# First query weights loaded in the key phase, the query products moved ahead of six value tiles, and their splits spread between value copies

## What is computed

```python
x = x + _L0_xattn_ref(_layernorm(x), ctx, ctx, Wq, Wk, Wv, Wd)
# inside: 32 query heads, 8 key/value heads, head size 128, 16 x 64 tokens, width 512
queries = _rope((q @ Wq.T).reshape(B, Sq, 32, 128).transpose(0, 2, 1, 3))
keys    = _rope((k @ Wk.T).reshape(B, Skv, 8, 128).transpose(0, 2, 1, 3))
values  = (v @ Wv.T).reshape(B, Skv, 8, 128).transpose(0, 2, 1, 3)
# then softmax(queries . keys) . values, times Wd, added to x
```

## Time and profile before

| | us |
|---|---|
| median of 3 runs (702.80 to 704.43) | 703.15 |
| the profiled execution | 705.12 |
| its span, first to last instruction | 703.1 |
| PE busy in that span | 693.3 (99%) |
| DVE busy | 517.9 (74%) |
| POOL busy | 471.2 (67%) |
| ACT busy | 371.7 (53%) |

### The profile page before, as it was taken

One profiled execution on the slowest core, in us unless ns is written; L12 is line 12 of the kernel. 1 busy time (PEld: TensorE's weight loads), 2 busy tenths in 40 slices (PEclk: granted clock), 3 DMA queues, 4 the chain that ended last, 5 costly groups with the idle time before them and its releaser, 6 DMA issues.

```text
span 703.1 us, 12868 instructions
## 1 busy us (share of the span) xinstructions
PE 693.3 (99%) x4841; PEld 563.6 (80%) x4841; DVE 517.9 (74%) x815; ACT 371.7 (53%) x560; POOL 471.2 (67%) x360
## 2 busy tenths in 40 slices
PE   8999999899999999999999999999999999999998
PEld 6887878678888888788788788887888888887886
DVE  5566898978768767767758758748658888899734
ACT  6356665734744743743752653654246777665220
POOL 2698155776787778778777877844525799985630
PEclk9999999999999999999999999999999999999999
DMA  7645513231310300311211212200300110010003
GB/s 264 213 151 176 163 61 89 91 141 43 116 49 16 134 30 27 122 45 48 87 45 60 75 45 76 76 16 2 104 2 1 46 32 32 2 64 29 16 1 119
DMA packets 25736, 51.08 MB, mean 73 GB/s; under 512 B 2400, under 2 KB 10720, under 8 KB 25696
## 3 DMA queue, kind: packets, MB, share of 16 engines
q1 hardware_dynamic: 25696, 50.53, 21.6%
HBM read 40.04 MB, written 10.49 MB: 72 GB/s over the span
## 4 chain that ended last, share of the span: by engine, by line
PE 85%; DVE 4%; POOL 4%; DMA 3%; issue 2%; ACT 1%; SPq 1%; POOLq 0%; DVEq 0%; ACTq 0%
PE pj L1733 13%; PE pj L1646 12%; PE pv L1733 10%; PE pj L1845 9%; PE tp L1646 9%; PE pj L2029 3%; PE pv L1632 3%; PE sc L1895 2%; PE tp L1908 2%; PE pv L1919 2%; PE pv L1720 2%; PE sc L1702 2%; PE tp L1709 2%; PE sc L1720 2%; POOL sm L506 2%
## 5 line engine op out<-in xcount | busy, mean ns | idle before, releaser
L500 POOL TENSOR_TENSOR sw<-sw,cst 128x512 f32<-128x512 f32 x72 | 97.0, 1347 | 41.9 <-ACT sw L685 41.7
L529 POOL TENSOR_TENSOR sm<-sm,rz 128x512 f32<-128x512 f32 x64 | 70.7, 1119 | 33.7 <-DVE rz L1259 33.7
L524 POOL TENSOR_TENSOR sm<-sm,mx 128x512 f32<-128x512 f32 x64 | 72.8, 1152 | 21.1 <-DVE mx L1253 13.4
L506 POOL TENSOR_TENSOR qr<-t,sw 128x512 f32<-128x512 f32 x54 | 73.8, 1367 | 7.8
L1646 PE MATMUL tp<-x,w 128*128 128x512 f32 x288 | 74.4, 395 | 0.0
L809 ACT ACTIVATE sm<-sm 128x512 f32<-128x512 f32 x64 | 40.1, 633 | 52.5 <-POOL sm L524 52.0
L518 POOL TENSOR_TENSOR w<-raw,w 128x896 fp32r<-128x896 f32 x24 | 50.3, 2117 | 25.9 <-ACT w L662 25.9
L1845 PE MATMUL pj<-xh,ws 128*128 128x512 f32 x192 | 64.6, 402 | 0.2 <-ACT kb L903 0.2
L1646 PEld LDWEIGHTS tp<-x,w 128*128 128x128 f32 x288 | 53.0, 188 | 10.7
L662 ACT ACTIVATE w<-raw 128x1792 fp32r<-128x1792 f32 x15 | 25.6, 1704 | 59.7 <-DVE raw L1113 59.7
L1257 DVE TENSOR_REDUCE zs<-sm 128x8 f32<-128x512 f32 x64 | 42.6, 666 | 14.0 <-ACT sm L809 13.7
(11 more groups left out here) (285 smaller groups left out, 1832.4 us busy)
## 6 DMA issues: line engine op xcount, KB each, us to landing
rawd<-in_w_d SPq DMA_DIRECT2D x16, 512.0 KB, 3.4
raw<-in_w_q SPq DMA_DIRECT2D x15, 512.0 KB, 3.3
kscr<-sm SPq DMA_DIRECT2D x16, 256.0 KB, 2.1
vscr<-sm SPq DMA_DIRECT2D x16, 256.0 KB, 2.6
kr<-kscr SPq DMA_DIRECT2D x8, 512.0 KB, 4.4
vv<-vscr SPq DMA_DIRECT2D x16, 256.0 KB, 3.4
raw<-in_w_v SPq DMA_DIRECT2D x4, 512.0 KB, 4.0
X<-in_x SPq DMA_DIRECT2D x4, 512.0 KB, 6.7
```

The costliest lines, as they stand in the source:

```text
L500: pool.tensor_tensor(bs(sw[par][:, :]), bs(sw[par][:, :]), rep(cst[:, C_SIN:C_SIN + S], HB), ALU.mult).then_inc(sin_done, 1)
L506: pool.tensor_tensor(o, bs(t1[par][:, :]), bs(sw[par][:, :]), ALU.add).then_inc(rope, 1)
L524: pool.tensor_tensor(s3, s3, per_group(mx[:, c, :], 8), ALU.subtract).then_inc(subbed, 1)
L529: pool.tensor_tensor(s3, s3, per_group(rz[:, c, :], 8), ALU.mult).then_inc(normed, 1)
```

## The change

It touches only the stretch up to the first head.

- The weights of query pair 0 are loaded into `raw8b` early, on SP's queue behind the loads of `X` and ahead of key pieces 4 and 5. Pair 1 then comes into `raw8`, pair 2 (`load_q(1, 0)`) into `raw8` too, so it waits for wlo 4 (both pairs split) where it waited for wlo 2.
- `PHASE1` ends behind value tile 9. Value tiles 10 to 15 stand behind the 14 products (before: 12 to 15).
- DVE: `stats_half(1)` comes one key tile earlier, the first two `ln_apply` three key tiles earlier, `w7_sum(0)` leaves the stretch between `ln_apply(5)` and `ln_apply(6)` and goes to key tile 7. The splits of weights and blocks behind it are put in another order. Both halves of `w7_lo(3, 1)` leave the first head and stand ahead of it, and `first_add(7)` stands ahead of `w7_sum(3)`.
- ACT: `w7_hi` and `block_hi` are spread over value copies 4 to 9.
- `t1f`'s third and fourth buffers lie in `kr` now, so `load_kr(0)` waits for all eight rope additions (rope Q0 + 8). It was free to load after wlo 4. The layer-norm temporaries move from `cq` to `swx`.

```diff
-         [("v", i) for i in range(5, 12)]
+         [("v", i) for i in range(5, 10)]
+V_LATE = 10
...
-        t1f, swf = t1 + [pt[0], t1x], sw + swx
+        t1f = t1 + [kr[:, i * HB:(i + 1) * HB, :].rearrange("p b s -> p (b s)") for i in range(2)]
...
             sp.dma_start(bthr[:, :], b_thr).then_inc(s_cols, 16)
+            load_q(0, 0, raw8b)
             for j in (4, 5):
...
-            sp.wait_ge(ln_t, NT)
-            load_q(0, 1, raw8b)
             for vi in range(6, NVT):
                 spill_v(vi)
                 if vi == 7:
-                    sp.wait_ge(wlo, 2)
-                    sp.wait_ge(wsum, 6)
+                    sp.wait_ge(wlo, 4)
                     load_q(1, 0)
                 if vi == 11:
                     for i in range(2):
                         sp.wait_ge(s_ks[i], 16 * NKT // 2)
-                    sp.wait_ge(wlo, 4)
-                    load_kr(0)
-                if vi == 12:
                     sp.wait_ge(wlo, 6)
                     load_q(1, 1)
+                    sp.wait_ge(rope, Q0 + 8)
+                    load_kr(0)
...
-                if ki in (5, 7):
-                    ln_pow((ki - 5) // 2)
+                if ki in (4, 5):
+                    ln_pow(ki - 4)
...
-                if ki in (3, 5):
-                    stats_half((ki - 3) // 2)
+                if ki in (3, 4):
+                    stats_half(ki - 3)
...
+                if ki == 7:
+                    w7_sum(0, raw8b)
...
+            for i in range(2):
+                w7_lo(0, 0, i, raw8b)
             block_lo(0)
...
+            w7_sum(1)
             block_lo(1)
-            w7_sum(1, raw8b)
             dve.wait_ge(ln_cp, NT)
             mix(0)
             mix(1)
-            for i in range(2):
-                w7_lo(1, 1, i, raw8b)
             block_lo(2)
             dve.wait_ge(tdone, 1)
             mix(2)
+            block_lo(3)
+            for i in range(2):
+                w7_lo(1, 1, i)
             dve.wait_ge(tdone, 3)
             mix(3)
+            block_lo(4)
             w7_sum(2)
-            block_lo(3)
-            block_lo(4)
...
             first_add(6, 6)
+            first_add(7, 7)
             w7_sum(3)
-            first_add(7, 7)
+            for i in range(2):
+                w7_lo(3, 1, i)
...
-                if first:
-                    w7_lo(3, 1, 0)
...
-                    w7_lo(3, 1, 1)
...
-            for i in range(12, NVT):
+            for i in range(V_LATE, NVT):
                 v_tile(i)
```

More of the change, by code:

```diff
@@ L121, in build @@
         wv1 = sb(p1, "wv1", [P, 2, KT, 512], F32R)
-        wk = [sb(p1, f"wk{i}", [P, 2, 2 * KT, P], F32R) for i in range(2)]
+        wk0 = sb(p1, "wk0", [P, 2, 2 * KT, P], F32R)
         sb(p1, "gap_p1", [P, 3 * 1024])
+        wk1 = sb(p1, "wk1", [P, 2, 2 * KT, P], F32R)
         wv0 = sb(p1, "wv0", [P, 2, KT, 512], F32R)
@@ L129, in build @@
         p1.close()
-        wv = [wv0, wv1]
+        wv, wk = [wv0, wv1], [wk0, wk1]
         f2 = ExitStack()
@@ L136, in build @@
         f2.close()
[L138 to L141, removed]
         pcb, u2b = sm4[0], sm4[1]
@@ L329, in ln_tmp @@
             if n < NT:
-                return cq[n % 2][:, :]
+                return swx[n % 2][:, :]
             return ((t1[1], sw[1], t1[0], sw[0]), sm4)[n // NT - 1][n % 4][:, :]
@@ L341, in build @@
         FIRST = [(0, 0), (1, 0), (0, 1), (1, 1), (0, 2), (1, 2), (0, 3), (1, 3)]
-        t1f, swf = t1 + [pt[0], t1x], sw + swx
+        t1f = t1 + [kr[:, i * HB:(i + 1) * HB, :].rearrange("p b s -> p (b s)") for i in range(2)]
+        swf = sw + swx
         block = es.enter_context(nc.Block())
@@ L408, in _ @@
                     sp.wait_ge(plo_d, 7)
-                    load_q(0, 0)
+                    sp.wait_ge(wsum, 1)
+                    load_q(0, 1)
                 if ki % 2 and ki >= 5:
                     spill_v((ki - 5) // 2)
-            sp.wait_ge(ln_t, NT)
-            load_q(0, 1, raw8b)
             for vi in range(6, NVT):
@@ L749, in _ @@
                     ln_copy(2 * (i - LN_AT) + 1)
-                if i == 5:
-                    block_hi(0)
-                    act.wait_ge(kproj, NKT)
[L753 to L761, removed]
+                if i == 4:
+                    act.wait_ge(kproj, 12)
+                    w7_hi(0, 0, raw8b, None)
+                elif i in (5, 6):
+                    block_hi(i - 5)
+                elif i == 7:
+                    block_hi(2)
+                    block_hi(3)
+                elif i == 8:
+                    act.wait_ge(kproj, NKT)
+                    w7_hi(1, 1, raw8, None)
+                elif i == 9:
                     block_hi(4)
@@ L798, in _ @@
             w7_hi(2, 0, raw8, 13)
+            v_copy(10)
+            first_swap(6, C_BANK, None, 3)
+            v_copy(11)
             v_copy(12)
-            first_swap(6, C_BANK, None, 3)
+            first_swap(7, T_BANK, None, 4)
             v_copy(13)
-            first_swap(7, T_BANK, None, 4)
+            w7_hi(3, 1, raw8, 14)
             v_copy(14)
             v_copy(15)
-            w7_hi(3, 1, raw8, 14)
             def exp(n, c, scale):
@@ L1151, in first_lo, with mix @@
                                   wk[0][:, 0, k, :].bitcast(F32), ALU.subtract).then_inc(s, 1)
+            def mix(i):
+                b11, b21, b22, b12 = xblock(0, 0), xblock(1, 0), xblock(1, 1), xblock(0, 1)
+                o, p, q = ((b11, b12, b11), (b12, b12, b22), (b22, b22, b11), (b21, b21, b22))[i]
+                dve.tensor_tensor(o, p, q, ALU.subtract).then_inc(tdone, 1)
             first_lo(0, phi_a, plo_a)
@@ L1164, in _ @@
                 t1_k(ki)
-                if ki in (3, 5):
-                    stats_half((ki - 3) // 2)
[L1167 to L1170, removed]
+                if ki in (3, 4):
+                    stats_half(ki - 3)
+                if ki in (3, 8):
+                    piece_lo({3: 4, 8: 5}[ki])
+                if ki in (6, 12, 14):
+                    n = {6: 0, 12: 2, 14: 4}[ki]
                     ln_apply(n)
                     ln_apply(n + 1)
-                if ki == 9:
-                    piece_lo(6)
-            w7_sum(0)
+                if ki == 7:
+                    w7_sum(0, raw8b)
+                if ki in (9, 11):
+                    piece_lo({9: 6, 11: 7}[ki])
             ln_apply(6)
             ln_apply(7)
[L1179 to L1182, removed]
+            for i in range(2):
+                w7_lo(0, 0, i, raw8b)
             block_lo(0)
-            for i in range(2):
-                w7_lo(0, 0, i)
+            w7_sum(1)
             block_lo(1)
-            w7_sum(1, raw8b)
             dve.wait_ge(ln_cp, NT)
```

## The result

The changed kernel took 706.87 us (median of 4 runs, 706.59 to 707.12) against 702.97 for the kernel before beside it: ratio 1.0044, 95% interval 1.003 to 1.0058. It is slower by 3.9 us; 705.9 was forecast, in a range of 702.8 to 707.8. On another chip the unedited pair gave 706.96 against 703.71, ratio 1.0052 (1.0038 to 1.0067).

A forecast was written before the change was run, and what follows sets the result against it. The prediction took the kernel as bound by PE, busy 693.3 of 703.1 us. Its terms, 0.8 + 3.2 + 1.7 - 2.9 = +2.8 us on the runs' median of 703.15, gave 705.9 us, range 702.8 to 707.8.

The forecast's parts named there:

- Part 1: Key phase: the early weight load delays the spill and POOL, making PE 0.8 us late from key tile 14 on.
- the engines are saturated, so 0.52 MB cost 1.3 us: Key phase: DMA engines at 410 GB/s, share 1.02, so the early load delays what is queued behind it by 1.3 us.
- the key tile near 37: Key phase: key tile 9 is free at 38.6 but PE wants it at 37.23, a wait of 1.4 us.
- Parts 2 and 3: Products: PE waits 1.4 us for pair 1's weights and 2.4 for first_swap(0); net +3.2 us.
- W: Ahead of pair 1's products: the time wlo 4 comes, with pair 1's weights split on DVE; forecast 87.4.
- the run of 16.2: DVE's work without a gap from ln_apply(6) at 71.2 to the end of w7_lo(1), forecast as 16.2 us.
- Part 4: Ahead of the first scores: load_kr(0) starts 14.3 us behind the products, so PE waits 1.7 us for kr (1.0 to 2.5).
- Part 5: First head: c_lo, wdl and pair 3's weights come earlier, so PE's waits there shrink: -2.9 us (-2.3 to -3.0).
- all of the 3.0 us: First head: the sum of PE's four waits there, of which the forecast gave all but 0.1 as gain.
- the head start is enough: Rival, products: pair 1 split by 83.5, so no waits for its weights or first_swap(0); 701.2 us, faster; chance 0.07.
- the new loads are hidden: Rival, loads up to the scores: shorter chain behind products, faster pair 2 load, free early load; 703.5 us, no difference; chance 0.18.
- the queue is worse: Rival, loads and head: kr's load takes its median, other loads cost more, head keeps 0.7 of waits; 708.2 us; chance 0.07.

The follow-up runs named there:

- e9: The kernel before, unedited, run for a second profiled execution: 703.03 us, span 701.1.
- e10: Kernel before with the change's head part alone (first_add(7) ahead of pair 3's sums, w7_hi(3, 1) earlier, w7_lo(3, 1) ahead of the first mask): ratio 1.003.
- e7: Changed kernel with the low halves of pair 0's weights ahead of ln_apply(6) and (7) on DVE: ratio 1.005 to the kernel before.
- e8: The changed kernel once more, unedited, on the other chip: ratio 1.0052 to the kernel before.
- e5: Changed kernel with pair 2's sums, w7_sum(2), issued behind first_t1(5) on DVE: ratio 1.0005 to the kernel before, 703.8 us.
- e3: Changed kernel with cosine products of first rows 6 and 7 kept in qr, so kr's load waits for rope Q0 + 4: ratio 1.0021 to the kernel before.
- e2: Changed kernel with ten extra 128x512 matmuls ahead of the product that waits for the first swap: ratio 1.0033 to the kernel before.
- e11: Changed kernel with the products behind twelve value tiles and four behind them: ratio 1.0055 to the kernel before.
- e12: The version with all four moves (e6), with the products behind twelve value tiles instead of ten: ratio 1.0045 to the kernel before.
- e4: Changed kernel with the head's part undone: pair 3's split and first_add(7) back where the kernel before has them. Ratio 1.0103 to the kernel before.
- e1: Changed kernel with pair 2's sums, w7_sum(2), issued behind block_lo(6) on DVE: ratio 1.0021 to the kernel before.
- e6: Changed kernel with the edits of e5, e3 and e7, and pair 3's sums ahead of first_add(7): 701.4 us, ratio 0.9967 to the kernel before.

## Why the prediction was right, and where it was off

The direction and the place of the loss were right, and the number was 1.0 us low. By its parts:

- **Part 1** (+0.8): it came out near its size, but not where the text put it. No key tile waited near 37. Against the execution of the earlier trace rows the products start 0.4 earlier, counting the two tiles fewer as 5.4, which looks like the lower bound of 0. Against e9 they start 0.84 later (82.20 + 5.44 - 86.80), and the trace has one stop for it:

```profile
60.87 0.63 PE L1576 MATMUL sc<-cst,swx 128*128 128x128 f32 x4 [0.82 <-DVE swx L1058]
```

The text took the wait of 0.7 behind `cq` in the earlier trace rows for a fixed part of the kernel before, whose place the new wait would only take. e9, and e10 with the same first phase, have no such wait. Of the eleven profiles of kernels with the change nine have it (0.55 to 0.82). The other two are e7 and e8, in which PE had stopped for 1.66 and 1.55 us in the first key tiles and came to this place later. In these nine POOL went on behind its wait for the spill at 29.32 to 29.94, in e9 at 28.90 and in e10 at 28.28 (30.09 in the earlier trace rows). A delay by the early load, carried on through POOL and DVE, would fit that, 0.4 to 1.0 us against e9 where the text has 1.3. But in e7 and e8 POOL went on at 28.88 and 28.45 with the same load ahead, and DVE's order changed too. No run takes the load alone away, so the cause of the 0.84 stays open.

The step that failed is "the engines are saturated, so 0.52 MB cost 1.3 us", and with it the key tile near 37. The saturation holds for 20 to 22; six us later the kernel before moved little, and part of the load fell there. DMA share and GB/s of 26 to 28, before and then after:

```profile
26.00:28.00 2.00, 2.00 (x11) 1.65 (x10) 1.70 (x7) 0.06 (x1) 0.00 (x0) 1.00 0.53 191
```

```profile
26.00:28.00 2.00, 2.00 (x10) 1.65 (x10) 1.27 (x3) 0.91 (x1) 0.00 (x0) 1.00 0.84 317
```

- **Parts 2 and 3**: the waits were forecast as 1.4 and 2.4 and came as 1.24 and 2.33, for the reasons given. W was 86.2 instead of 87.4: `ln_apply(6)` began at 70.18 instead of 71.2, and the run of 16.2 from there took 16.0. e5 shows the second chain by taking it away.
- **Part 4** (wait of 1.7 for `kr`): 1.19, or 1.9 where the clock stayed full; e3 removes it. What the text did not see is how much this wait levels. The scores started at 124.37 to 124.98 in five executions of four kernels (after, e8, e2, e7, e11), whatever PE had lost before: a late start, 1.5 us of half clock, products behind ten or twelve tiles. The parts of the sum ahead of `kr` were not additive; the chain that ends in `kr`'s load was the bound, and it follows the products' end only loosely.
- **Part 5** (-2.9): it measured -3.9. From the first scores to the scores of the next group it is 172.51 - 118.74 = 53.77 us before and 174.27 - 124.45 = 49.82 after, though the idle times in the rows add up to 2.98 only. Each of the four waits cost about 0.25 more than its bracket: a matmul's row is 0.39 long where the next starts 0.23 behind it, so the first 0.16 of a stop does not show as idle time. The other 0.3 of the difference is not explained. The mis-sized term is "all of the 3.0 us".
- **The base**: I added +2.8 to the median, but worked the terms out on an execution of before that had lost 1.9 us ahead of the scores. The change seems to lose nothing by such a late start, since its waits take it up: in e8 the products start 1.08 us later than in after, and the scores at 124.37. Against e9 the account is +7.6 at the scores (0.9 for the later end of the products, 5.5 for two more tiles behind them, 1.2 for `kr`) and -3.9 in the head: +3.7, for 3.9 and 3.3 measured. The forecast had +5.7 and -2.9. Its 124.5 for the scores' start was right to 0.05 us; what it was compared with was not.
- **Luck**: that the 124.5 fits so well is chance in part. The text had the products from 83.3 to 106.3 and the scores 18.2 behind them. They ran from 82.20 to 106.79, with the scores 17.7 behind. The half clock (1.5), which the text lacks, stands against an earlier start (1.1) and a shorter chain behind the products (0.5). e8 comes nearer, with 83.28, 106.00 and 18.4, but its 83.28 stems from the stop in the first key tiles. And as the wait for `kr` levels what comes ahead of it, the fit says less about the single steps than it seems to. In the total, 1.9 us too little ahead of the head and 1.0 us too little gain in it leave an error of 1.0.

The rival "the head start is enough" fell with W = 86.2, "the new loads are hidden" with the wait for `kr`; "the queue is worse" came nearest in time, but not by its terms.

## What to carry to other kernels

Moving work of the bounding engine changes nothing by itself; look for the one chain that ends last at the next junction (here: last weights, rope, free `kr`, load) and ask whether the move shortens it. A wait on a late load belongs behind everything in that queue that does not need it, and its new place has to be checked for what stands behind it there. A gain that rests on cover must be tried with the cover it will have, and the terms should be added to more than one execution of the kernel before.

## What the hardware showed beyond that

**The clock behind a pause.** Pauses of PE of 2.33 (after and e12), 2.35 (e4), 2.34 (e7), 2.38 (e11) and 3.87 us (e10) were followed by a granted clock of 0.50. Pauses of 2.21 (e8), 2.51 (e3) and 2.74 us (e1) were not, nor were those of 1.8 to 2.1 us at `kr` and at the value tiles (e2, e4, e5, e8, e12). So near 2.3 us it comes in some executions and not in others. The length of the pause is not all that counts. Among the first key tiles, where PE had done only two matmuls since the warm-up (5.32 to 6.02), a pause of 1.55 us brought it in e8:

```profile
7.57 2.73 PE L1618 MATMUL pj<-cxh,wk 128*128 128x512 f32 x6 [1.55 <-ACT cxh L658]
```

```profile
8.00:10.00 2.00, 2.00 (x6) 1.45 (x5) 2.00 (x4) 1.43 (x3) 0.00 (x0) 0.54 1.03 398
```

One of 1.66 us did the same in e7, behind six matmuls (clock 0.50 from 10 to 12 us). So e7's expectation, that a pause of 1.5 leaves the clock at 1.00, does not hold everywhere.

In e5 and e6, whose profiles show no pause of PE above 1.9, 20 of 21 executions had a mean clock of 0.999 or 1.0; of after's nine, two. In after the later wait for `kr` takes the loss up: its scores start within 0.1 us of those of e8, which had the full clock there. In e1, which has no wait behind it, the three executions at 1.0 took 704.6 to 705.8 and the nine at 0.998 took 705.8 to 706.7. That these nine lost it behind the pause of 2.74 was not seen, only argued; e8 shows that a lower mean can come from the start.

**DVE beside POOL.** A 128x256 sum took 0.43 us with POOL idle and 1.51 beside its rope; two 128x896 subtractions 2.08 and 3.18. The Trainium skill (GPSIMD Engine Reference, Specifications) says that GpSimd shares its SBUF interfaces with VectorE and that VectorE instructions with two SBUF inputs contend with it; by that rule all of these do, and the trace agrees.
